# In an attention unit, the turned probabilities are put ahead of the scores two units on, and their low halves ahead of the maximum

## The chip, the core and the metric

One NeuronCore of a Trainium2 chip runs the whole program. It has five engines, each with an instruction stream of its own: TensorE (PE in the rows, its weight loads PEld), VectorE (DVE), ScalarE (ACT), GpSimd (POOL) and SyncE (SP), which here issues the transfers. The engines meet only at semaphores. The metric is the device time of one execution in microseconds. The kernel before takes 1871.24 us, the median of 2 runs (1870.88 to 1871.59).

## What is computed

A graph network on 1250 nodes with 512 features, 21,250 edges: four transformer blocks with attention along the edges, then a two-layer graph convolution. Of the reference, cut to what the change touches:

```python
def _sparse_attention(x, src, dst, wq, bq, wk, bk, wv, bv, wo, bo):
    q = (x @ wq + bq).reshape(N, H, Dh) * Dh ** (-0.5)      # H = 4 heads of Dh = 128
    k = (x @ wk + bk).reshape(N, H, Dh)
    v = (x @ wv + bv).reshape(N, H, Dh)
    scores = jnp.einsum('ehd,ehd->eh', q[src], k[dst])
    smax = jax.ops.segment_max(scores, src, num_segments=N)
    ex = jnp.exp(scores - smax[src])
    denom = jax.ops.segment_sum(ex, src, num_segments=N)
    attn = ex / denom[src]
    out = jax.ops.segment_sum(attn[:, :, None] * v[dst], src, num_segments=N)
    return out.reshape(N, D) @ wo + bo
for i in range(4):
    x = x + _sparse_attention(cond_layer_norm(x), ...)      # the change is here
    x = x + mlp(cond_layer_norm(x))
```

## The kernel before

The edges are turned into a dense 1250 x 1250 table once (how often an edge occurs, as a bias in the logarithm), so that attention is dense: scores plus bias, a softmax along the row, and a product with V. Products are made in three passes from a high and a low half of each operand (fp32r), which is why nearly every tile has a "low half" that VectorE or GpSimd makes by a subtraction.

**Units.** One unit is one head of one tile of 125 query rows. A group G has two tiles and four heads, so 8 units (k = 0 to 7, head k // 2, tile k % 2); a layer has 5 groups, so 40 units, and four layers have 160. What a unit k takes, by engine:

- TensorE, scores: 9 matmuls from q and k into three PSUM banks (`scores`, operands qg and kT, recorded at the helper line L1690).
- VectorE, `score_max`, L1272: adds the bias tile `bt`, writes the sum to SB (pbuf in a few units) and the row maximum to `nmx`, in one custom instruction with a short read of the accumulator behind it.
- ScalarE, `exp_unit`, L870: the exponential of 125x1250 elements, with its row sum `den`.
- VectorE, `normalise`, L1277, L1279, L1281: two instructions on one column (dmx, rden) and the scaling of the 125x1250 probabilities in `P` (pbuf in the rows).
- TensorE, `turn_probs`, L1790: 10 transposes of those probabilities into three further banks.
- ScalarE, `turn_out`, L876: three copies out of these banks, the high half of PT. VectorE, `turn_low`, L1288: three subtractions, the low half.
- TensorE, `attend` (operands PT and V, also L1690): half of a head's 30 matmuls beside each unit; then ScalarE's copy `attn_out` (outTg, L881) and VectorE's `out_low` (outTl, L1294), once per head.

After a group's last head TensorE multiplies with the output weights (`attn_project`, operand WOS), and VectorE adds the two tiles to z (`attn_add`, L1301).

**What sets the order.** Nothing is scheduled automatically: each engine's list is written out by hand, and each engine takes its list in order. All of them work at two units at once: beside unit k, the scores of unit n = k + 2. The five groups of a layer are one loop on each engine (`attn_rest`, then `attn_first` of the next group; four passes) with a start before it and an end, `attn_end`, behind. The waits that matter are few:

```python
# score_max(n): S(n) has been made, and the exponential of unit n-1 has read SB
# normalise(n):
dve.wait_ge(s["exp"], U + 1)            # the exponential of the same unit
# turn_low(k), per piece:
dve.wait_ge(s["Thi"], 3 * U + i + 1)    # ScalarE's copy of the same piece
# scores(n) on TensorE:
pe.wait_ge(s["ttr"], AHEAD + U)         # the maximum of unit n-1 has read the banks
# turn_probs(k) on TensorE:
pe.wait_ge(s["P"], U + 1)               # k is normalised
pe.wait_ge(s["Te"], AHEAD + 3 * U)      # turn_low(k-1) has read the banks
```

ScalarE's list is `turn_out(k)`, `exp_unit(k + 2)` and, at odd k, `attn_out`; the change leaves it alone. VectorE's `attn_end` writes its last units out singly, and has `turn_low` of unit 5 ahead of `score_max` of unit 7 already.

Of the kernel before, what the change touches and what calls it, by code (L numbers as in the profile page):

```python
# [41 lines left out]
UNITS = 2 * H  # L42
# [17 lines left out]
def build(nc, x, src, dst, node_vec1, f_w1, f_b1, f_w2, f_b2, s1_w, s1_b, b1_w, b1_b, wq, bq, wk, bk, wv, bv,  # L60
# [5 lines left out]
    with ExitStack() as ctx:  # L66
# [219 lines left out]
        def settled(eng):  # L286


            eng.sem_inc(s["settled"], 1)
# [743 lines left out]
        def _(dve):  # L1033
# [230 lines left out]
            def score_max(G, U, u, first=False, own=True, banks=ps_S):  # L1264
                dve.wait_ge(s["S"], U + 1)
                dve.wait_ge(s[f"st{u}"], 32 * (G + 1))
                if own:
                    dve.wait_ge(s["exp"], U)
                elif not first:
                    dve.wait_ge(s["Tp"], AHEAD + (3 * (U - 1)))  # L1270
                settled(dve)
                v.tensor_tensor_reduce(out=SB[:, :] if own else P[:, u, :], in0=banks, in1=bt[:, u, :], scale=-1.0, scalar=FLOOR,  # L1272
                                       op0=ALU.add, op1=ALU.min, accum_out=nmx[:, u:u + 1]).then_inc(s["ttr"], 1)

            def normalise(U, u):
                dve.wait_ge(s["exp"], U + 1)
                v.tensor_scalar(dmx[:, u:u + 1], den[:, u:u + 1], 1e-30, None, ALU.max).then_inc(s["dmx"], 1)  # L1277
                dve.wait_ge(s["dmx"], U + 1)
                v.reciprocal(rden[:, u:u + 1], dmx[:, u:u + 1]).then_inc(s["rden"], 1)  # L1279
                dve.wait_ge(s["rden"], U + 1)  # L1280
                v.tensor_scalar(P[:, u, :], P[:, u, :], rden[:, u:u + 1], None, ALU.mult).then_inc(s["P"], 1)  # L1281

            def turn_low(U, h, u):

                for i, (a, b) in enumerate(PIECES):
                    dve.wait_ge(s["Thi"], 3 * U + i + 1)
                    o = PT[:, h % 2, :, a:b, u * T:(u + 1) * T]
                    v.tensor_tensor(o[:, 1], ps_T[0:T, i, 0:(b - a) * T].rearrange("p (t n) -> p t n", n=T),  # L1288
                                    o[:, 0].bitcast(F32), ALU.subtract).then_inc(s["Te"], 1)
# [27 lines left out]

            def unit(G, k, last):
                n = k + 2
                score_max(G + n // UNITS, UNITS * G + n, n % 2, False, not (last and k == 4))  # L1320
                turn_low(UNITS * G + k, k // 2, k % 2)
                normalise(UNITS * G + n, n % 2)

            def attn_first(l, g_):
                for k in range(2):
                    unit(l * NC + g_, k, False)
                    if k == 0:
                        out_low(l * NC + g_ - 1, H - 1)
                attn_add(l, g_ - 1)

            def attn_rest(l, g_):
                for k in range(2, UNITS):
                    unit(l * NC + g_, k, False)
                    if k % 2:
                        out_low(l * NC + g_, k // 2 - 1)

            def attn_end(l, f2):
                G = l * NC + NC - 1
                U = UNITS * G
                for k in range(2, 5):  # L1340
                    unit(G, k, True)
                    if k % 2:
                        out_low(G, k // 2 - 1)
                turn_low(U + 5, 2, 1)
                score_max(G, U + 7, 1, False, False)
                dve.wait_ge(s["zB"], AHEAD + 2 * NC * l + 2)
                front_stats(f2, 0)
                out_low(G, 1)
                turn_low(U + 6, 3, 0)
                normalise(U + 7, 1)  # L1350
                dve.wait_ge(s["Tp"], AHEAD + 3 * (U + 7))
                front_norm(f2, 0)
                out_low(G, 2)
                turn_low(U + 7, 3, 1)
                dve.wait_ge(s["Tp"], AHEAD + 3 * (U + 8))
                front_mod(f2)
                out_low(G, 3)
# [229 lines left out]
        def _(pe):  # L1587
# [182 lines left out]
            def scores(G, U, h, u):  # L1770
                pe.wait_ge(s["qg"], AHEAD + (H * G + h + 1))
                pe.wait_ge(s["ttr"], AHEAD + U)
                for a, b in COLS:
                    e = product(psf[0:T, a:b], lambda i: qg[:, i, h, u * T:(u + 1) * T], lambda i: kT[:, i, h, a:b], True, True)
                e.then_inc(s["S"], 1)
# [7 lines left out]
            def turn_probs(U, u, first=False):  # L1783
                if first:
                    pe.wait_ge(s["ttr"], AHEAD + U + 2)
                pe.wait_ge(s["P"], U + 1)
                pe.wait_ge(s["Te"], AHEAD + 3 * U)
                for p, (a, b) in enumerate(PIECES):
                    for m in range(a, b):
                        e = turn(ps_T[0:T, p, (m - a) * T:(m - a + 1) * T], P[:, u, m * T:(m + 1) * T], ident[0:T, 0:T])  # L1790
                    e.then_inc(s["Tp"], 1)
# [14 lines left out]

            def unit(G, k, last):
                n = k + 2
                if n < UNITS or not last:
                    scores(G + n // UNITS, UNITS * G + n, n % UNITS // 2, n % 2)  # L1810
                turn_probs(UNITS * G + k, k % 2)

            def attn_first(G):

                unit(G, 0, False)
                attend(G - 1, H - 1, 2)
                unit(G, 1, False)
                attn_project(G - 1)

            def attn_rest(G, begun=False):  # L1820
                for k in range(2, UNITS):
                    if begun and k == 2:
                        attend(G, 0, 0)
                        unit(G, k, False)
                    else:
                        unit(G, k, False)
                        attend(G, k // 2 - 1, k % 2)
# [200 lines left out]
```

## Time and profile before

| what | value |
|---|---|
| median of the runs | 1871.24 us (1870.88 to 1871.59) |
| the profiled execution | 1871.84 us |
| its span, first to last instruction | 1870.1 us |
| PE busy | 1810.0 us, 97% |
| PE weight loads busy | 1575.5 us, 84% |
| DVE busy | 1382.6 us, 74% |
| ACT busy | 826.5 us, 44% |
| POOL busy | 453.8 us, 24% |
| granted TensorE clock | 0.996 of full speed |

Busy time is that of instructions on the engine; waiting for a semaphore isn't in it. Attention takes about 214 us in each of the four layers (in the second, from the first maximum at 644.16 us to the last low half of the outputs at 858.19 us).

### The profile page before, as it was taken

The page shows a single profiled execution, that of the slowest core. Times are in us where ns is not written, and L with a number is a line of the kernel's source. Part 1 is how long each engine was busy: PE and PEld are TensorE (multiplying, and loading weights), DVE is VectorE, ACT ScalarE, POOL GpSimd, SP SyncE. Part 2 cuts the span into 40 slices and gives each one's busy share as a digit, 9 for nine tenths or more (in the row PEclk, how much of TensorE's full clock was granted, in tenths as well). Part 3 has the DMA queues.
Part 4 walks back from the last instruction along what each step waited for, and adds up shares of the span by engine and source line. Part 5 has one row for each costly group of instructions (what it writes and reads, how often), then busy time and mean ns, then how long its engine had stood idle before and what let it go on. Part 6 is the DMA issues. An engine that isn't in the chain of part 4 may idle for free. (4 is left out here: it accounts for less than half of the span.)

```text
span 1870.1 us, 33910 instructions
## 1 busy us (share of the span) xinstructions
PE 1810.0 (97%) x11814; PEld 1575.5 (84%) x11814; DVE 1382.6 (74%) x2847; ACT 826.5 (44%) x1613; POOL 453.8 (24%) x547
## 2 busy tenths in 40 slices
PE   6988999999999999999999999999999999999999
PEld 4656988999789889998898899988998999887877
DVE  8996668888875588888754988888549888885431
ACT  1552465555432255554322545544226545536220
POOL 2000333112341341113413411125134111262000
PEclk9999999999999999999999999999999999999999
DMA  4213462110300111113011211040112110522001
GB/s 143 55 41 79 141 176 91 38 43 27 123 24 34 58 42 39 38 31 124 4 54 42 58 38 38 27 128 1 46 50 61 38 38 27 142 72 55 1 1 55
DMA packets 50755, 108.43 MB, mean 58 GB/s; under 512 B 18170, under 2 KB 18222, under 8 KB 50640
## 3 DMA queue, kind: packets, MB, share of 16 engines
q1 hardware_dynamic: 50608, 106.87, 19.7%
q8 instruction: 73, 1.20, 0.3%
q14 instruction: 42, 0.34, 0.1%
q0 software_dynamic: 32, 0.03, 0.0%
HBM read 83.62 MB, written 23.25 MB: 57 GB/s over the span
## 5 line engine op out<-in xcount | busy, mean ns | idle before, releaser
L876 ACT ACTIVATE PT<-ps 125x500 fp32r<-125x500 f32 (+1 forms) x480 | 214.3, 520 | 315.1 <-PE ps L1790 315.1
L1690 PE MATMUL ps<-PT,V 125*128 125x250 f32 x2400 | 313.2, 284 | 1.7 <-DVE PT L1288 1.7
L1690 PE MATMUL ps<-kT,qg 128*125 128x512 f32 (+1 forms) x1440 | 302.1, 354 | 6.3 <-DVE nmx L1272 5.6
L1690 PEld LDWEIGHTS ps<-kT,qg 128*125 128x125 f32 x1440 | 245.4, 186 | 56.0 <-issue 6.9
L1690 PEld LDWEIGHTS ps<-PT,V 125*128 125x128 f32 x2400 | 289.6, 190 | 2.9 <-DVE PT L1288 2.9
L1288 DVE TENSOR_TENSOR PT<-ps,PT 125x500 fp32r<-125x500 f32 (+1 forms) x480 | 253.1, 582 | 2.1 <-ACT PT L876 1.7
L1272 DVE CUSTOM_DVE_ANT_0 SB<-ps,bt 125x1250 f32<-125x1250 f32 x140 | 203.9, 1457 | 47.4 <-PE ps L1690 44.6
L1790 PE MATMUL ps<-ident,pbuf 125*125 125x125 f32 x1600 | 202.2, 273 | 9.9 <-DVE PT L1288 4.0
L1790 PEld LDWEIGHTS ps<-ident,pbuf 125*125 125x125 f32 x1600 | 187.2, 189 | 13.6 <-issue 8.8
L870 ACT ACTIVATE pbuf<-SB,nmx 125x1250 f32<-125x1250 f32 x140 | 188.1, 1344 | 12.1 <-DVE nmx L1272 10.4
L1281 DVE TENSOR_SCALAR pbuf<-pbuf,rden 125x1250 f32<-125x1250 f32 x160 | 150.1, 938 | 5.6
L543 POOL CAST qg<-qc 128x250 fp32r<-128x250 f32 x80 | 36.4, 454 | 443.1 <-PE ps L1690 408.3
L1690 PEld LDWEIGHTS ps<-yTb,wa 128*128 128x128 f32 x1152 | 136.8, 189 | 3.1 <-issue 1.3
L1690 PE MATMUL ps<-yTb,wa 128*128 128x250 f32 x1152 | 137.3, 279 | 1.1 <-DVE yTb L1237 1.1
L1690 PE MATMUL ps<-wmS,hT 128*125 128x512 f32 x480 | 124.3, 403 | 3.8 <-POOL hT L614 3.4
L1632 PE MATMUL ps<-oh_src,oh_dst 125*125 125x512 bf16 (+1 forms) x576 | 115.4, 358 | 6.9 <-DVE oh_src L1116 6.9
L1690 PEld LDWEIGHTS ps<-yT,wmS 128*128 128x128 f32 x960 | 115.6, 191 | 4.2 <-issue 2.4
L1690 PE MATMUL ps<-yT,wmS 128*128 128x250 f32 x960 | 116.0, 280 | 2.0 <-DVE yT L1237 2.0
L1632 PEld LDWEIGHTS ps<-oh_src,oh_dst 125*125 125x125 bf16 x576 | 71.1, 142 | 53.3 <-DVE oh_src L1116 26.0
L1690 PEld LDWEIGHTS ps<-wmS,hT 128*125 128x125 f32 x480 | 84.4, 186 | 32.6 <-POOL hT L614 11.5
L1116 DVE TENSOR_SCALAR oh_src<-iota,edgeT 125x1250 bf16<-125x1250 f16 x192 | 103.7, 540 | 0.0
L1690 PE MATMUL ps<-WOS,outTg 128*125 128x512 f32 x320 | 102.2, 400 | 0.3
(246 smaller groups left out, 2811.6 us busy)
## 6 DMA issues: line engine op xcount, KB each, us to landing
bt<-edge_bias_scratch SPq DMA_DIRECT2D x40, 546.9 KB
q_scratch<-qc SPq DMA_DIRECT2D x16, 500.0 KB, 2.6
qc<-q_scratch SPq DMA_DIRECT2D x16, 500.0 KB, 4.8
counts_scratch<-cblk SPq DMA_DIRECT2D x10, 546.9 KB
c_rows<-counts_scratch SPq DMA_DIRECT2D x10, 546.9 KB
edge_bias_scratch<-b_rows SPq DMA_DIRECT2D x10, 546.9 KB
counts<-counts_scratch SPq DMA_DIRECT2D x10, 546.9 KB
wm<-in_L_gnn_wo_dram SPq DMA_DIRECT2D x4, 1024.0 KB, 8.6
```

What stands on the lines that cost most here:

```text
L543: g.tensor_copy(qg[:, 0, h, :], qc[:, h, :]).then_inc(s["qgh"], 1)
L870: sc.activation(P[:, u, :], SB[:, :] if own else P[:, u, :], ACT.Exp, bias=nmx[:, u:u + 1], scale=-1.0, accum_out=den[:, u:u + 1]).then_in ...
L876: sc.activation(PT[:, h % 2, 0, a:b, u * T:(u + 1) * T], ps_T[0:T, i, 0:(b - a) * T].rearrange("p (t n) -> p t n", n=T), ACT.Copy).then_in ...
L1116: v.tensor_scalar(oh_src[:, slot, :], iota16[:, :], edgeT[:, 0, bass.ds(chunk0 + b, 1)], None, ALU.is_equal).then_inc(s[f"onehot{ring}"], 1)
L1272: v.tensor_tensor_reduce(out=SB[:, :] if own else P[:, u, :], in0=banks, in1=bt[:, u, :], scale=-1.0, scalar=FLOOR, op0=ALU.add, op1=ALU.m ...
L1281: v.tensor_scalar(P[:, u, :], P[:, u, :], rden[:, u:u + 1], None, ALU.mult).then_inc(s["P"], 1)
L1288: v.tensor_tensor(o[:, 1], ps_T[0:T, i, 0:(b - a) * T].rearrange("p (t n) -> p t n", n=T), o[:, 0].bitcast(F32), ALU.subtract).then_inc(s[ ...
L1632: e = mm(psf[0:T, o + a:o + b], oh_dst[:, slot, 0:T], oh_src[:, slot, a:b], start=False, stop=False, skip_group_check=True)
L1690: e = mm(out_, lhs(a), rhs(b), start=start and i == 0, stop=stop and i == 2)
L1790: e = turn(ps_T[0:T, p, (m - a) * T:(m - a + 1) * T], P[:, u, m * T:(m + 1) * T], ident[0:T, 0:T])
```

## The change

Two lines change places, on two engines. On TensorE, beside unit k, the probabilities of k are turned first and the scores of k + 2 made behind them. On VectorE the low halves of unit k are made first, then the maximum of unit k + 2, and directly behind it the normalising of k + 2. No instruction is added or removed, and none changes its shape; waits keep their conditions and move with their instructions.

```diff
@@ VectorE
             def unit(G, k, last):
                 n = k + 2
+                turn_low(UNITS * G + k, k // 2, k % 2)
                 score_max(G + n // UNITS, UNITS * G + n, n % 2, False, not (last and k == 4))
-                turn_low(UNITS * G + k, k // 2, k % 2)
                 normalise(UNITS * G + n, n % 2)
@@ TensorE
             def unit(G, k, last):
                 n = k + 2
+                turn_probs(UNITS * G + k, k % 2)
                 if n < UNITS or not last:
                     scores(G + n // UNITS, UNITS * G + n, n % UNITS // 2, n % 2)
-                turn_probs(UNITS * G + k, k % 2)
```

VectorE in the loop over groups, unit 3, as it stood (L1272 the maximum and its read, L1286 and L1288 the low halves with their waits, L1277 to L1281 the normalising):

```order
L1265 REGISTER_ALU
L1272 ISA SB,nmx<-ps,bt 125x1250
L1272 ISA nmx 125x1
L1286 ISA
L1288 TENSOR_TENSOR PT<-ps,PT 125x4x125
L1286 REGISTER_ALU
L1288 TENSOR_TENSOR PT<-ps,PT 125x4x125
L1286 REGISTER_ALU
L1288 TENSOR_TENSOR PT<-ps,PT 125x2x125
L1277 TENSOR_SCALAR dmx<-den 125x1
L1279 RECIPROCAL rden<-dmx 125x1
L1281 TENSOR_SCALAR pbuf<-pbuf,rden 125x1250
```

The same unit on VectorE now:

```order
L1286 ISA
L1288 TENSOR_TENSOR PT<-ps,PT 125x4x125
L1286 REGISTER_ALU
L1288 TENSOR_TENSOR PT<-ps,PT 125x4x125
L1286 REGISTER_ALU
L1288 TENSOR_TENSOR PT<-ps,PT 125x2x125
L1265 REGISTER_ALU
L1272 ISA SB,nmx<-ps,bt 125x1250
L1272 ISA nmx 125x1
L1277 TENSOR_SCALAR dmx<-den 125x1
L1279 RECIPROCAL rden<-dmx 125x1
L1281 TENSOR_SCALAR pbuf<-pbuf,rden 125x1250
```

The three low halves stood between the read of the maximum and the first instruction of the normalising; now nothing stands there.

TensorE at the head of the loop, unit 2, as it stood (L1772 and L1787 are waits, L1790 the transposes, L1796 and L1798 the waits of the product with V):

```order
L1690 MATMUL ps<-kT,qg 125x512 x6
L1690 MATMUL ps<-kT,qg 125x226 x3
L1786 REGISTER_ALU
L1787 ISA
L1790 MATMUL ps<-ident,pbuf 125x125 x10
L1796 ISA
L1798 ISA
L1690 MATMUL ps<-PT,V 128x250 x15
```

The same on TensorE now:

```order
L1787 ISA
L1790 MATMUL ps<-ident,pbuf 125x125 x10
L1771 ISA
L1772 REGISTER_ALU
L1690 MATMUL ps<-kT,qg 125x512 x6
L1690 MATMUL ps<-kT,qg 125x226 x3
L1796 ISA
L1798 ISA
L1690 MATMUL ps<-PT,V 128x250 x15
```

Transposes, scores, product: the cycle is the same ring of three, with the transposes and the scores exchanged.

## Rows read from the trace of the kernel before

**Rows 1.** The page, busy time by engine: us (share of span) xinstructions

```profile
PE 1810.0 (97%) x11814; PEld 1575.5 (84%) x11814; DVE 1382.6 (74%) x2847; ACT 826.5 (44%) x1613; POOL 453.8 (24%) x547
```

**Rows 2.** Windows: stretch, length, busy PE, PEld, DVE, ACT, POOL, clock, DMA, GB/s

```profile
702.00:744.00 42.00, 42.00 (x298) 38.64 (x297) 35.97 (x71) 22.75 (x45) 6.99 (x10) 1.00 0.15 43
0.00:46.00 46.00, 31.06 (x141) 19.32 (x141) 37.70 (x130) 7.34 (x9) 9.82 (x23) 0.96 0.48 146
```

**Rows 3.** Timeline, VectorE in the loop: start us, us, instruction, [idle before <-releaser]

```profile
701.76 1.46 DVE L1272 CUSTOM_DVE_ANT_0 SB<-ps,bt 125x1250 f32<-125x1250 f32 x1 [1.16 <-PE ps L1690]
703.14 0.08 DVE L1272 DVE_READ_ACCUMULATOR2_ANT nmx<- 125x1 f32 x1
703.14 1.58 DVE L1288 TENSOR_TENSOR PT<-ps,PT 125x500 fp32r<-125x500 f32 x3
704.72 0.15 DVE L1277 TENSOR_SCALAR dmx<-den 125x1 f32<-125x1 f32 x1
705.11 0.87 DVE L1281 TENSOR_SCALAR pbuf<-pbuf,rden 125x1250 f32<-125x1250 f32 x1
...
718.65 1.10 DVE L1281 TENSOR_SCALAR pbuf<-pbuf,rden 125x1250 f32<-125x1250 f32 x1
719.67 0.41 DVE L1294 TENSOR_TENSOR outTl<-ps,outTg 128x250 fp32r<-128x250 f32 x1
720.00 1.44 DVE L1272 CUSTOM_DVE_ANT_0 SB<-ps,bt 125x1250 f32<-125x1250 f32 x1
```

**Rows 4.** Timeline, ScalarE in the same stretch

```profile
703.26 1.34 ACT L870 ACTIVATE pbuf<-SB,nmx 125x1250 f32<-125x1250 f32 x1
...
706.39 1.34 ACT L876 ACTIVATE PT<-ps 125x500 fp32r<-125x500 f32 x3 [1.70 <-PE ps L1790]
```

**Rows 5.** Timeline, TensorE in the same stretch

```profile
704.05 1.87 PE L1690 MATMUL ps<-kT,qg 128*125 128x512 f32 x9
705.76 1.25 PE L1790 MATMUL ps<-ident,pbuf 125*125 125x125 f32 x10
...
708.62 1.89 PE L1690 MATMUL ps<-kT,qg 128*125 128x512 f32 x9
```

**Rows 6.** Timeline, the end of one pass and the start of the next

```profile
735.96 0.71 PE L1690 MATMUL ps<-WOS,outTg 128*125 128x512 f32 x2
...
741.62 1.87 PE L1690 MATMUL ps<-kT,qg 128*125 128x512 f32 x9
742.02 0.69 DVE L1301 TENSOR_TENSOR z<-ps,z 125x512 f32 x1 [1.87 <-PE ps L1690]
...
743.87 1.46 DVE L1272 CUSTOM_DVE_ANT_0 SB<-ps,bt 125x1250 f32<-125x1250 f32 x1 [1.16 <-PE ps L1690]
```

**Rows 7.** Timeline, start of the second layer's attention: unit 3's maximum, exponential, normalising

```profile
657.27 0.08 DVE L1272 DVE_READ_ACCUMULATOR2_ANT nmx<- 125x1 f32 x1
...
657.39 1.34 ACT L870 ACTIVATE pbuf<-pbuf,nmx 125x1250 f32<-125x1250 f32 x1 [1.70 <-DVE nmx L1272]
...
658.85 0.15 DVE L1277 TENSOR_SCALAR dmx<-den 125x1 f32<-125x1 f32 x1 [0.33 <-ACT pbuf L870]
...
660.26 1.45 DVE L1272 CUSTOM_DVE_ANT_0 SB<-ps,bt 125x1250 f32<-125x1250 f32 x1
```

**Rows 8.** Timeline, VectorE at the end of that layer's attention

```profile
827.94 1.46 DVE L1272 CUSTOM_DVE_ANT_0 SB<-ps,bt 125x1250 f32<-125x1250 f32 x1 [1.00 <-PE ps L1690]
...
842.89 1.59 DVE L1288 TENSOR_TENSOR PT<-ps,PT 125x500 fp32r<-125x500 f32 x3 [0.43 <-ACT PT L876]
844.39 1.45 DVE L1272 CUSTOM_DVE_ANT_0 pbuf<-ps,bt 125x1250 f32<-125x1250 f32 x1
```

**Rows 9.** Timeline, TensorE early in the program, three matmuls of one kind twice

```profile
13.82 1.30 PE L1620 MATMUL ps<-zeros 125*125 125x512 bf16 x3 [2.99 <-DVE tab L1093]
...
28.34 0.72 PE L1620 MATMUL ps<-zeros 125*125 125x512 bf16 x3
```

## The prediction, made before the changed kernel had run

> **What bounds the kernel now.** I read the page's busy times first: TensorE at 97%, VectorE at 74% [rows 1]. An average can't say what a reordering is worth, so I went to one pass of the attention loop, 8 units. From the first maximum of one pass at 701.76 [rows 3] to that of the next at 743.87 [rows 6] it takes 42.1 us. In 42.0 us of it TensorE is busy throughout, VectorE 35.97 us [rows 2]. Inside the pass TensorE goes from scores to scores in 708.62 - 704.05 = 4.57 us [rows 5]. VectorE's idle time is spent waiting for it: 1.16 us ahead of the first maximum [rows 3, 6], 1.87 us ahead of the second addition to z [rows 6]. So TensorE sets the pace, and VectorE has 6.0 us of slack in a pass, 0.75 us a unit.
>
> Then I looked at what fills VectorE between a maximum and its own unit's normalising. The read of the maximum is at 703.14, the exponential starts at 703.26 [rows 4], and dmx at 704.72: 1.58 us. The three low halves lie in just this gap, also 1.58 us [rows 3]. That the gap is a wait and not their length is seen at the start of a layer, where no low halves stand there: maximum read 657.27, exponential 657.39, dmx 658.85, again 0.12 + 1.46 = 1.58 us, the last 0.33 us of it idle with the exponential as the releaser [rows 7].
>
> **The change, on VectorE.** It takes the low halves out of that gap and puts them ahead of the maximum. VectorE takes its list in order, so normalising k + 2 waits out the exponential of k + 2 with nothing to do, and the low halves of k + 1 stand behind it. One unit, link by link:
>
> - low halves to maximum: 1.50 us (842.89 to 844.39, where one directly follows the other [rows 8]; each starts 0.08 us before the other ends);
> - maximum to its read: 1.38 us; read to dmx: 1.58 us; dmx to the scaling of P: 0.39 us (704.72 to 705.11) [rows 3];
> - scaling to the next instruction: 0.79 us, its 0.87 less 0.08, the overlap seen at 718.65 (1.10 long, next at 1.02) [rows 3].
>
> That is 5.64 us, against TensorE's 4.57. Eight units are 45.1; a pass also has four low halves of outputs at 0.33 us (719.67 to 720.00 [rows 3]), 1.3, and two additions to z at 0.69 - 0.08, 1.2. Together 47.6 us: VectorE becomes the bound.
>
> **On TensorE** no time is added: transposes, scores and product take the same 4.57 us in the other order, and each finds its input. Turning unit k + 1 needs the low halves of k, done 1.5 us into VectorE's 5.64; the scores need the maximum before, done before that. It idles about 1.1 us a unit, which costs nothing. **ScalarE** copies the turned probabilities of k + 1 only behind the exponential of k + 2. From the exponential's start that is 1.34, plus one piece at 1.34 / 3 = 0.45 [rows 4], and at odd units at most 0.4 for the copy of the outputs: 2.2 us, while VectorE asks for the piece after 1.46 + 0.39 + 0.79 = 2.64. No wait, with 0.4 us to spare.
>
> **At the end of a pass** the cover is thinner. The product with the output weights starts some 0.5 us after the last low half of outputs began and takes 741.62 - 735.96 = 5.66 us [rows 6]. The transposes behind it start at 6.16, ScalarE's first copy 0.63 later (705.76 to 706.39 [rows 4, 5]), ready at some 7.4. VectorE comes to these low halves at 0.33 + 1.50 + 3.35 + 0.79 + 1.22 = 7.2: a wait of 0.2. The scores start 1.0 after the transposes, and the maximum can start 2.25 behind them (741.62 to 743.87 [rows 6]), at 9.4, where VectorE would be at 8.9: 0.5 more. A pass is then 48.3 us, 6.2 more than now.
>
> **Per layer.** Three such passes give 18.6. The first pass now takes 701.76 - 660.26 = 41.5 [rows 3, 7], so it gains 6.8. At its start a maximum followed the scaling at once; now low halves come first: 1.5, the exchange itself. At the end three units run from 827.94 to 844.39, 16.45 us [rows 8]; as changed they are 3 x 5.64 + 0.33 = 17.25, plus 0.8. Behind that point VectorE's list is as it was. Sum 27.7 us, four layers 111 us. The profiled execution's 1871.84 becomes 1982.8, and the median of the runs lies 0.6 below it: **1983 us**.
>
> No queue of transfers is moved past anything. The next group's bias tiles and queries are asked for by the same maxima and scores, now further apart, so they have more time. The granted clock is 1.00 in the pass [rows 2].
>
> **What is least known** is the handover from low halves to maximum, since the row has a maximum of the kind without the wait for SB. From above I bound it by a start 0.10 us after the low halves' end in place of 0.08 us before: 0.18 x 35 units x 4 = 25 us more. I take the row, since the maximum at 720.00, with all its waits, also starts 0.08 us early [rows 3]. From below: without the waits at pass ends, 0.7 x 16 = 11 us less, and 3 less for roundings of 0.02 us a unit. GpSimd's work can stretch the scaling from 0.87 to 1.10 [rows 3]: once a pass, 4 us. So the likeliest case spans 1968 to 2012.
>
> **Rivals.** (1) *The most occupied engine stays the bound.* Place: VectorE's gap behind each maximum. Had the exponential been done when VectorE arrives, or were the wait up to 0.75 us, it would fit into VectorE's slack, and TensorE's 42.1 us a pass would stand: 1871 us. For it: TensorE is 97% busy, and its work is the same. The Trainium skill ("Perfetto Trace Analysis", section "Identifying the Most-Contended Engine") takes the engine with the highest occupancy as the bottleneck, for TensorE by its weight loads, here 84% against VectorE's 74%; by that rule the time would stay at 1871. Against it: the wait is 1.58 us twice over in the rows [rows 3, 7], and 8 x 1.58 = 12.6 us doesn't fit into 6.0. Even if all slack were used, 6.6 us x 16 passes remain. I give it 4%.
>
> (2) *ScalarE's copies come late too.* Place: the low halves of k + 1 wait for the copy behind the exponential. It decides if ScalarE's chain is over 0.4 us longer than the rows add up to. With another 0.4 us in each of 140 units: 56 us, 2039. Against it, the copies and the exponential hold their lengths closely. 6%.
>
> (3) *TensorE, now idle in each unit, loses its clock.* Three matmuls take 1.30 us where they come out of 2.99 us of idling and 0.72 later [rows 9], 1.8 times as long, so at 1.2 GHz in place of 2.4. A pass would be up to 42.1 x 1.8 = 76 us, and 16 passes add up to 540 us: about 2410. It decides if TensorE at 42.1 / 48.3 = 87% busy isn't enough. Against it: in the first 46 us TensorE is busy for 31.06, 68%, at a granted 0.96 [rows 2]. The Trainium skill ("TensorE: Matmul & The Clock Gate", section "Part 1: The HAM clock gate (the "warmup" mystery)") has a unit that watches how busy the array is and gates it to half rate when it idles; by that rule this case is real wherever idling counts as enough. 3%.
>
> **Chances and range.** The likeliest case has 87%. The range 1965 to 2013 takes in its bounds; outside lie rival (3), rivals (1) and (2), and a little of the first case. A run of this kernel tells 2% (37 us) from no change with ease. Faster by over 2%: nothing in attention can go below TensorE's 42.1 us a pass, 1%. Within 2%: rival (1), 4%. Slower by over 2%: 95%.
>
> **What would show it.** In the changed kernel's timeline: dmx 1.58 us behind every read of a maximum, with VectorE idle before it and the exponential as releaser, some 140 times; maxima 5.6 us apart (6.0 across an output's low half) in place of 4.6; a pass of 48 us; TensorE's busy share down to about 92% of the span; a granted clock still at 1.00. Wrong it would be if VectorE had other work in the gap, if the low halves waited for ScalarE in every unit, or if the scores were the late ones: then the wait ahead of the maximum would name TensorE inside the pass and not only at its ends.

## The result, and the profile after

The changed kernel takes **1995.34 us** (median of 2 runs, 1994.56 to 1996.11) against 1871.24 before: a ratio of 1.0667, 95% interval 1.065 to 1.0684. It is slower by 124 us; 1983 was forecast, with a range of 1965 to 2013. The profiled execution has a span of 1992.8 us, 122.7 more than before.

The page's busy times of the changed kernel, in the form of [rows 1]:

```profile
PE 1857.1 (93%) x11814; PEld 1593.9 (80%) x11814; DVE 1376.0 (69%) x2847; ACT 817.2 (41%) x1613; POOL 456.2 (23%) x547
```

Nothing in these shares says that VectorE is now the bound: its share has fallen from 74% to 69%, and TensorE is still the busiest engine. It is so inside a pass too: of the 48.39 us from 742.28 to 790.67, TensorE is busy for 44.86 and VectorE for 35.18. The loop's timeline says what the shares don't. VectorE of the changed kernel, one unit and the start of the next (start us, us, instruction, idle before and releaser):

```profile
705.52 1.45 DVE L1272 CUSTOM_DVE_ANT_0 SB<-ps,bt 125x1250 f32<-125x1250 f32 x1
706.89 0.08 DVE L1272 DVE_READ_ACCUMULATOR2_ANT nmx<- 125x1 f32 x1
708.47 0.15 DVE L1277 TENSOR_SCALAR dmx<-den 125x1 f32<-125x1 f32 x1 [1.50 <-ACT pbuf L870]
...
708.86 0.87 DVE L1281 TENSOR_SCALAR pbuf<-pbuf,rden 125x1250 f32<-125x1250 f32 x1
709.65 1.58 DVE L1288 TENSOR_TENSOR PT<-ps,PT 125x500 fp32r<-125x500 f32 x3
711.14 1.45 DVE L1272 CUSTOM_DVE_ANT_0 SB<-ps,bt 125x1250 f32<-125x1250 f32 x1
```

Between the read of the maximum at 706.89 and dmx at 708.47 lie 1.58 us, as in [rows 3, 7], but now 1.50 us of it are idle, with the exponential as releaser. The low halves come after the scaling, and from maximum to maximum it is 711.14 - 705.52 = 5.62 us, against TensorE's 4.57 before [rows 5]. ScalarE, with the copies of the turned probabilities directly behind the exponential:

```profile
755.37 1.34 ACT L870 ACTIVATE pbuf<-SB,nmx 125x1250 f32<-125x1250 f32 x1 [3.03 <-DVE nmx L1272]
756.61 0.19 ACT L870 ACTIVATION_READ_ACCUMULATOR pbuf<-SB,nmx 125x1 f32 x1
756.70 1.31 ACT L876 ACTIVATE PT<-ps 125x500 fp32r<-125x500 f32 x3
```

TensorE in the same stretch of the loop; its idle time, named in brackets, is what VectorE leaves it:

```profile
754.01 1.35 PE L1790 MATMUL ps<-ident,pbuf 125*125 125x125 f32 x10 [0.83 <-DVE PT L1288]
755.38 1.98 PE L1690 MATMUL ps<-kT,qg 128*125 128x512 f32 x9
```

The waits, summed over the whole program (us in total, times, longest us):

```profile
ACT pbuf L870 <- DVE nmx L1272: 453.1, 152, 5.3
DVE dmx L1277 <- ACT pbuf L870: 211.7, 146, 1.5
PE ps L1790 <- DVE PT L1288: 66.2, 77, 2.0
ACT PT L876 <- PE ps L1790: 59.0, 36, 3.8
```

The second line is the change: 211.7 us of VectorE's time in 146 waits, most of 1.5 us. It is more than the 124 us lost, since before VectorE had slack in every unit, and part of the new wait used that up. The first and third lines are engines waiting for VectorE. ScalarE's long wait for TensorE's transposes, 315.1 us before, has shrunk to 59.0.

The end of a pass, VectorE, to be read beside [rows 6]:

```profile
738.76 1.28 DVE L1301 TENSOR_TENSOR z<-ps,z 125x512 f32 x2
740.20 1.59 DVE L1288 TENSOR_TENSOR PT<-ps,PT 125x500 fp32r<-125x500 f32 x3 [0.16 <-ACT PT L876]
742.28 1.46 DVE L1272 CUSTOM_DVE_ANT_0 SB<-ps,bt 125x1250 f32<-125x1250 f32 x1 [0.49 <-PE ps L1690]
...
790.67 1.46 DVE L1272 CUSTOM_DVE_ANT_0 SB<-ps,bt 125x1250 f32<-125x1250 f32 x1 [0.49 <-PE ps L1690]
```

The two short waits of 0.2 and 0.5 us stand where they were expected, and the pass takes 790.67 - 742.28 = 48.4 us, 42.1 before.

### The profile page after: what moved, and what is told of

It reads as the page before. It is cut to its first block and busy times, and to the rows that moved or that the text cites. A ratio compares the mean times of both kernels' runs of the same rounds, so it can differ in the third digit from the quotient of the medians.

```text
span 1992.8 us, 33910 instructions
## 1 busy us (share of the span) xinstructions
PE 1857.1 (93%) x11814; PEld 1593.9 (80%) x11814; DVE 1376.0 (69%) x2847; ACT 817.2 (41%) x1613; POOL 456.2 (23%) x547
## 5 line engine op out<-in xcount | busy, mean ns | idle before, releaser
L1690 PE MATMUL ps<-kT,qg 128*125 128x512 f32 (+1 forms) x1440 | 317.4, 365 | 4.4 <-DVE nmx L1272 1.9
L1690 PE MATMUL ps<-PT,V 125*128 125x250 f32 x2400 | 303.3, 280 | 1.6 <-DVE PT L1288 1.6
L1790 PE MATMUL ps<-ident,pbuf 125*125 125x125 f32 x1600 | 214.3, 282 | 77.7 <-DVE PT L1288 66.2
L1790 PEld LDWEIGHTS ps<-ident,pbuf 125*125 125x125 f32 x1600 | 192.2, 192 | 97.5 <-DVE PT L1288 44.1
L1288 DVE TENSOR_TENSOR PT<-ps,PT 125x500 fp32r<-125x500 f32 (+1 forms) x480 | 252.8, 582 | 3.3 <-ACT PT L876 2.9
L1272 DVE CUSTOM_DVE_ANT_0 SB<-ps,bt 125x1250 f32<-125x1250 f32 x140 | 203.2, 1451 | 8.7 <-PE ps L1690 8.3
L1277 DVE TENSOR_SCALAR dmx<-den 125x1 f32<-125x1 f32 x160 | 24.6, 153 | 211.7 <-ACT pbuf L870 211.7
L543 POOL CAST qg<-qc 128x250 fp32r<-128x250 f32 x80 | 42.7, 533 | 535.1 <-PE ps L1690 507.5
L1281 DVE TENSOR_SCALAR pbuf<-pbuf,rden 125x1250 f32<-125x1250 f32 x160 | 153.5, 959 | 5.6
```

The lines of the kernel that those rows point to most:

```text
L543: g.tensor_copy(qg[:, 0, h, :], qc[:, h, :]).then_inc(s["qgh"], 1)
L1690: e = mm(out_, lhs(a), rhs(b), start=start and i == 0, stop=stop and i == 2)
```

## The experiments

Each ratio is to the kernel before on the same chip, with its 95% interval. That kernel took 1870.38 us beside e1 to e4 and 1868.69 us beside e5 to e8, so a difference between one of these times and 1995.34 holds to about 3 us.

**One half of the change at a time.** `e1_dve_only` is the VectorE part of the diff alone, `e2_pe_only` the TensorE part alone.

```diff
 # e1, VectorE (TensorE as before)
+                turn_low(UNITS * G + k, k // 2, k % 2)
                 score_max(G + n // UNITS, UNITS * G + n, n % 2, False, not (last and k == 4))
-                turn_low(UNITS * G + k, k // 2, k % 2)
 # e2, TensorE (VectorE as before)
+                turn_probs(UNITS * G + k, k % 2)
                 if n < UNITS or not last:
                     scores(G + n // UNITS, UNITS * G + n, n % UNITS // 2, n % 2)
-                turn_probs(UNITS * G + k, k % 2)
```

> The change on VectorE alone; TensorE keeps scores, then transposes. Theory A (an engine's list is a ring: what stands between a unit's maximum and its normalising is idle time, and each exchange lengthens a ring): VectorE still waits 1.58 us behind each maximum, and the low halves of k, now ahead of the maximum of k+2, also wait for the transposes that TensorE makes only behind the scores. The ring scores 1.71, transposes to ScalarE's copy 0.63, first piece 0.6, low halves 1.50, maximum to its read 1.38 plus 0.1 is 5.9 us a unit, some 50.5 us a pass: 2030 us, slower than both changes together. Rival B (only VectorE's gap counts, TensorE's order doesn't matter): as the whole change, 1995 us. Rival C (TensorE's reordering is what costs): near 1871.

Measured: 2050.15 us, ratio 1.0956 (1.0938 to 1.0974). Slower than both changes together, as theory A had it, and 20 us more than it said. The ring can be read off VectorE, TensorE and ScalarE of e1:

```profile
764.24 1.45 DVE L1272 CUSTOM_DVE_ANT_0 SB<-ps,bt 125x1250 f32<-125x1250 f32 x1
765.61 0.08 DVE L1272 DVE_READ_ACCUMULATOR2_ANT nmx<- 125x1 f32 x1
...
765.75 1.99 PE L1690 MATMUL ps<-kT,qg 128*125 128x512 f32 x9 [1.27 <-DVE nmx L1272]
...
767.57 1.26 PE L1790 MATMUL ps<-ident,pbuf 125*125 125x125 f32 x10
...
768.21 1.34 ACT L876 ACTIVATE PT<-ps 125x500 fp32r<-125x500 f32 x3 [0.79 <-PE ps L1790]
...
768.83 1.59 DVE L1288 TENSOR_TENSOR PT<-ps,PT 125x500 fp32r<-125x500 f32 x3
770.34 1.45 DVE L1272 CUSTOM_DVE_ANT_0 SB<-ps,bt 125x1250 f32<-125x1250 f32 x1
```

Maximum, scores, transposes, copy, low halves, maximum: 1.51 + 1.82 + 0.64 + 0.62 + 1.51 = 6.10 us. The expectation had 5.9. Of the 0.2 us between them 0.11 is that it took the scores at 1.71, their length when they follow other work; behind an idle time they take 1.82 here. A pass is 51.4 us (maxima at 758.14 and 809.52), 50.5 expected. VectorE waits for the exponential as long as in the changed kernel, 211.8 us in all against 211.7, so the 55 us between the two don't lie in that wait but in the longer ring through TensorE.

> The change on TensorE alone; VectorE keeps maximum, low halves, normalising, so there is no gap behind the maximum. Theory A (rings): the maximum of k+2 now waits for scores that stand behind the transposes of k, and the transposes of k+1 wait for the low halves of k, which VectorE makes behind that maximum: transposes 1.01, scores to maximum 2.10, to its read 1.38, low halves 1.50 plus 0.1 is 6.1 us a unit, 51.6 us a pass: 2045 us, with dmx finding the exponential nearly done. Rival B (only VectorE's gap costs): 1871 us. Rival C (the change's whole cost is TensorE's): 1995 us.

Measured: 2077.12 us, ratio 1.111 (1.1092 to 1.1129), the slowest of all, again in A's direction and 32 us over its number. On VectorE of e2 dmx comes 1.58 us behind the read of the maximum, with the low halves in between, and the wait stands ahead of the maximum instead:

```profile
742.63 0.08 DVE L1272 DVE_READ_ACCUMULATOR2_ANT nmx<- 125x1 f32 x1
742.63 1.58 DVE L1288 TENSOR_TENSOR PT<-ps,PT 125x500 fp32r<-125x500 f32 x3
744.21 0.15 DVE L1277 TENSOR_SCALAR dmx<-den 125x1 f32<-125x1 f32 x1
...
747.63 1.46 DVE L1272 CUSTOM_DVE_ANT_0 SB<-ps,bt 125x1250 f32<-125x1250 f32 x1 [2.16 <-PE ps L1690]
```

and on TensorE of e2:

```profile
744.36 1.32 PE L1790 MATMUL ps<-ident,pbuf 125*125 125x125 f32 x10 [1.68 <-DVE PT L1288]
745.45 1.96 PE L1690 MATMUL ps<-kT,qg 128*125 128x512 f32 x9
```

Low halves to transposes 1.73, to scores 1.09, to the maximum 2.18, to its read 1.38: 6.38 us, where 6.1 had been added up, and a pass is 53.0 us, 51.6 expected. So the change isn't a gap on VectorE plus something harmless on TensorE: each half alone makes a longer ring than the two together. With TensorE's half beside it, VectorE's half costs a ring of 5.62 us instead of 6.10.

**Taking the gap away.** `e3_norm_late` leaves both exchanges in and normalises one unit later; the start and the end of a layer are fitted to it (normalising of unit 3 into the loop, that of unit 6 behind the last low halves of unit 5).

```diff
 # VectorE, on the changed kernel
                 turn_low(UNITS * G + k, k // 2, k % 2)
+                normalise(UNITS * G + k + 1, (k + 1) % 2)
                 score_max(G + n // UNITS, UNITS * G + n, n % 2, False, not (last and k == 4))
-                normalise(UNITS * G + n, n % 2)
```

> Both exchanges stay; VectorE normalises unit k+1 between the low halves of k and the maximum of k+2, so its exponential is long done and the 1.5 us gap is gone. Theory A (rings through in-order lists): ScalarE still copies the turned k+1 only behind the exponential of k+2, so the low halves of k+1 now wait: maximum to exponential 1.50, exponential 1.34, first piece 0.6, low halves 1.50, normalising 1.18 is 6.1 us a unit: 2045 us, the wait moved from dmx to the low halves. Rival B (the gap on VectorE is all that costs): VectorE's list is 4.1 us a unit, TensorE's 4.57 us sets the pace again, near 1875 us.

Measured: 2046.16 us, ratio 1.0944 (1.0925 to 1.0962). VectorE's gap is gone and the time has risen by 51 us. The waits of e3 (us in total, times, longest us) show where it went:

```profile
DVE outTl L1294 <- ACT outTg L881: 126.8, 72, 1.8
PE ps L1790 <- DVE pbuf L1281: 122.1, 95, 2.2
DVE PT L1288 <- ACT PT L876: 119.0, 76, 2.0
```

In nearly every unit VectorE now waits for a copy of ScalarE: for that of the output where an output's low half comes first (126.8 us in 72 waits, the largest), else for that of the turned probabilities (119.0 us in 76). Both copies stand in ScalarE's list behind the exponential of k + 2, whose maximum VectorE has only just made. The maxima are 6.10 us apart, 6.1 expected, and 6.37 across an output. Rival B falls: removing the visible wait alone buys nothing.

`e4_norm_exp_late` adds the matching shift on ScalarE; the start and the end of a layer are again fitted to it.

```diff
 # ScalarE, on e3
                 turn_out(UNITS * G + k, k // 2, k % 2)
-                exp_unit(UNITS * G + k + 2, k % 2, not (last and k == 4))
+                exp_unit(UNITS * G + k + 1, (k + 1) % 2)
```

> As the one before, and ScalarE's list shifted too: the exponential of k+1 behind the copies of k, so each copy stands ahead of the next exponential. Theory A: ring of scaling to transposes 0.97, to the copy 0.63, copies 1.34, exponential to dmx 1.46, dmx to scaling 0.39 is 4.8 us a unit, 43.9 us a pass, with a somewhat slower start of each layer: 1912 us, four per cent faster than the change and two slower than before, VectorE no longer idle behind the maximum. Rival B (some other wait of the new order, PSUM banks between transposes and low halves, holds it at 5.6 us or more): 1990 us or over.

Measured: 1911.82 us, ratio 1.0226 (1.0209 to 1.0243), where 1912 was expected. The exponential of the next unit now stands behind the copies:

```profile
770.25 1.45 DVE L1272 CUSTOM_DVE_ANT_0 SB<-ps,bt 125x1250 f32<-125x1250 f32 x1
...
771.20 1.34 ACT L876 ACTIVATE PT<-ps 125x500 fp32r<-125x500 f32 x3 [2.16 <-PE ps L1790]
...
771.82 1.59 DVE L1288 TENSOR_TENSOR PT<-ps,PT 125x500 fp32r<-125x500 f32 x3
...
772.41 1.35 ACT L870 ACTIVATE pbuf<-SB,nmx 125x1250 f32<-125x1250 f32 x1
...
773.88 0.15 DVE L1277 TENSOR_SCALAR dmx<-den 125x1 f32<-125x1 f32 x1 [0.47 <-ACT pbuf L870]
...
775.05 1.45 DVE L1272 CUSTOM_DVE_ANT_0 SB<-ps,bt 125x1250 f32<-125x1250 f32 x1
```

A unit takes 4.80 us, and VectorE waits 0.47 us where it waited 1.50. So the two exchanges need not cost 6.7%: two of the three lists had been moved and the third had not. It is still 2% behind the kernel before, where TensorE's own 4.57 us a unit set the pace.

**Changing the length of the wait.** In `e5_after_exp_half` (on the changed kernel) and `e6_before_exp_half` (on the kernel before) the exponential of 140 units covers 625 of 1250 columns; the rest of each row keeps old values, and the row sum is held at 1 or more.

```diff
+                w = N // 2 if own else N
-                sc.activation(P[:, u, :], SB[:, :] if own else P[:, u, :], ACT.Exp, ...
+                sc.activation(P[:, u, 0:w], SB[:, 0:w] if own else P[:, u, :], ACT.Exp, ...
```

> The changed kernel with the exponential of 140 of the 160 units over 625 of the 1250 columns, and the row sum held at 1 or more; the rest of the row keeps old values. Theory A (VectorE waits out the exponential in every unit): the exponential shortens by some 0.6 us (0.36 us for 250 columns, 1.34 for 1250), the gap from the read of the maximum to dmx from 1.58 to some 0.97, and the time by somewhat less than 140 x 0.61, since the ends of the passes wait for TensorE instead: 1915 us. Rival B (the gap is a fixed handover or the slower pace comes from elsewhere): no more than 5 us off 1995.

Measured: 1929.8 us, ratio 1.0316 (1.0299 to 1.0334); 1915 was expected. The gap shrinks to 1.06 us, as VectorE and ScalarE of e5 show:

```profile
739.99 0.08 DVE L1273 DVE_READ_ACCUMULATOR2_ANT nmx<- 125x1 f32 x1
...
740.11 0.82 ACT L871 ACTIVATE pbuf<-SB,nmx 125x625 f32<-125x625 f32 x1 [2.98 <-DVE nmx L1273]
...
741.05 0.15 DVE L1278 TENSOR_SCALAR dmx<-den 125x1 f32<-125x1 f32 x1 [0.98 <-ACT pbuf L871]
```

That is 0.52 us a unit, not 0.61. 140 x 0.52 would be 73 us; 1995.34 - 1929.8 = 65.5 us are saved. The last unit of a pass gains nothing, since there VectorE waits for the product with the output weights (the last maxima of a pass are 7.70 us apart, at 760.02 and 767.72, and 7.65 to 7.69 in the changed kernel): 16 x 0.52 = 8 us less. (Some 5 us of the 65.5 are another matter: the stretched scalings described below happen to be shorter in e5.) The time follows the exponential's length, so the wait for it is part of VectorE's pace.

> The same shorter exponential in the kernel before, where the low halves fill the gap and TensorE sets the pace. Theory A: nothing gained in the loop, at most some 3 us at the ends of the layers: 1868 to 1871 us. Rival B (the exponential is on the path in both orders): some 80 us less, 1790.

Measured: 1871.34 us, ratio 1.0009 (1.0 to 1.0019): no change. The same work off the same instruction is worth 65.5 us in one order and nothing in the other, since there the low halves cover it.

**Filling the gap.** `e7_gap_filled`: on the changed kernel, `out_low` of a head stands between `score_max` and `normalise`, and ScalarE's `attn_out` ahead of `exp_unit`.

```diff
                 score_max(G + n // UNITS, UNITS * G + n, n % 2, False, not (last and k == 4))
+                if low is not None:
+                    out_low(*low)
                 normalise(UNITS * G + n, n % 2)
```

> The changed kernel with the low half of a head's output put between the read of the maximum and dmx, and ScalarE's copy of it ahead of the exponential. Theory A (work is free in the gap): 0.33 us off VectorE's 5.97 us at four units of a pass, one to two us a pass with the waits at its end: 46.6 us a pass and some 1968 us. Rival B (the copy ahead of the exponential delays it by as much as the gap gives back): no change from 1995.

Measured: 1967.6 us, ratio 1.0526 (1.0508 to 1.0543), 28 us less than the change, where 1968 was expected; a pass is 46.7 us, 46.6 expected. VectorE of e7:

```profile
740.03 0.08 DVE L1269 DVE_READ_ACCUMULATOR2_ANT nmx<- 125x1 f32 x1
740.03 0.41 DVE L1291 TENSOR_TENSOR outTl<-ps,outTg 128x250 fp32r<-128x250 f32 x1
...
741.61 0.15 DVE L1274 TENSOR_SCALAR dmx<-den 125x1 f32<-125x1 f32 x1 [1.17 <-ACT pbuf L870]
```

The low half of the output takes none of VectorE's time here; dmx is still 1.58 us behind the read.

**GpSimd beside the scaling.** `e8_bias_small` leaves out GpSimd's addition of the output bias for all but 2 of 512 columns.

```diff
-                    g.tensor_tensor(z_i, z_i, bob[:, :], ALU.add).then_inc(s["zb"], 1)
+                    g.tensor_tensor(z_i[:, 0:2], z_i[:, 0:2], bob[:, 0:2], ALU.add).then_inc(s["zb"], 1)
```

> The changed kernel with GpSimd's addition of the output bias to z over 2 of 512 columns. Theory A (GpSimd's work stretches VectorE's scaling of P, and VectorE's list now sets the pace): the four scalings of 2.0 us (one per layer, beside this addition in a layer's last pass) go back to 0.87, 4 x 1.15 = 4.6 us less: 1991 us, the other stretched ones stay. Rival B (the stretched scalings are coincidence, or their time is made up elsewhere): 1995 us, and 2.0 us rows stay.

Measured: 1991.43 us, ratio 1.0649 (1.0631 to 1.0666). The 3.9 us to the changed kernel are no more than the two intervals allow by chance, so the rows decide. In the changed kernel, fourth pass of the second layer, GpSimd and then VectorE:

```profile
855.98 5.02 POOL L567 TENSOR_TENSOR z<-z,bob 125x512 f32 x4
```

```profile
859.63 2.04 DVE L1281 TENSOR_SCALAR pbuf<-pbuf,rden 125x1250 f32<-125x1250 f32 x1
```

The same scaling in e8:

```profile
858.11 0.87 DVE L1281 TENSOR_SCALAR pbuf<-pbuf,rden 125x1250 f32<-125x1250 f32 x1
```

That pass takes 48.2 us in e8 and 49.4 in the changed kernel. All four scalings beside this addition are back at 0.87 us; the other stretched ones stay, the longest at 2.00 us.

## Why the prediction held, and where it was 12 us short

**The bound changed as forecast.** VectorE's 5.64 us a unit was added up from five links read off the trace before and measured at 5.62 to 5.64. The pass was 48.3 forecast, 48.4 measured, its two end waits included. The signs named are there: 146 waits of dmx, TensorE's share at 93%; only the granted clock didn't stay at 1.00 throughout. TensorE idles 3.5 us in a pass, where the forecast left it 6.2: its transposes and scores take longer beside the idle times, 1.35 and 1.98 us in the rows above for 1.25 and 1.89 before. (The forecast's last step has a slip: 1982.8 less 0.6 is 1982.2, not 1983.)

**The handover called least known**, low halves to maximum, is 1.49 us (709.65 to 711.14), 1.50 as taken, so the upper bound's 25 us were not needed.

**Too small was the stretched scaling.** I had it once a pass at 0.23 us, 4 us in all, and only in the range. The scalings' busy time over 160 units is 153.5 us where 160 x 0.872 is 139.5: 14.0 us of stretching, in 20 scalings, five of them at 2.0 us. Before it was 10.6 us in 32, most of it covered by TensorE. On the new bound nearly all of it counts: in the second layer 0.93 us in the first pass, 1.17 in the fourth, 0.48 and 0.52 in the end, 3.1 us, and 0.36 more in the start. The second layer's attention takes 31.7 us more than before, where 27.7 had been added up, so stretching is 3.5 of the 4.0 us missed there. The four attentions together take 125.2 us more; the rest of the program takes 2.5 us less, most of it behind the last layer's attention and unexplained, and that gives the 122.7 on the spans against 111 forecast. e8 shows for the largest kind that the stretching comes from GpSimd's work beside the scaling; for the others the trace has only that GpSimd is busy beside each of them.

**The rivals.** (1), the most occupied engine stays the bound, is refuted by e5 and e6: the exponential counts on the path in the new order only. TensorE has the highest share in both kernels, by matmuls (93% against 69%) and by weight loads (80%), and VectorE sets the pace in the loop. The Trainium skill's rule ("Perfetto Trace Analysis", section "Identifying the Most-Contended Engine") names TensorE here, and the measurement goes the other way: an engine that waits in its own list sets the pace at a falling share. (2), ScalarE's copies late in every unit, didn't happen in the change: in the loop the first piece is ready 1.91 us behind the exponential's start and VectorE asks for it after 2.64, or 2.18 and 2.97 beside an output. ScalarE had 0.7 to 0.8 us to spare and not 0.4; the prediction had counted the copy of the output on ScalarE's side and not its low half on VectorE's. e3 shows what the rival's mechanism costs where VectorE does come too early: 2046 us. (3), the clock, happened in spots, below.

**What e1 and e2 missed.** They came out 20 and 32 us above their sums. A pass is 0.9 and 1.4 us longer than added up, 14 and 22 us over 16 passes. The 6 and 10 us that are left are about what falls of the granted clock cost, which no sum had. Five units of e1 hold such a fall. One of them, in the second layer, has its scores at half rate behind a wait of 3.12 us (shown in the last section) and takes 7.74 us; in the first layer the same unit, behind the same wait but without a fall, takes 6.16. Together the five take 7.7 us more than their neighbours. In e2 there are four, one in the first pass of each layer, of 7.8 to 8.9 us where the others take 6.4: 8 us more, with no unit in that place without a fall to compare them with. In both kernels TensorE is on the ring, so a fall costs time at once.

## What to carry to other kernels

When an engine takes its list in order, ask what stands between an instruction and the next one that needs another engine's answer to it: that is cover. Moving it leaves the engine idle for the answer's round trip once per unit, here 1.50 us, and all of that but the engine's slack is lost, whatever its share of busy time. Add up the ring through all lists before moving a step in one of them. Here the exchange costs 9.6% on VectorE's list alone, 11.1% on TensorE's alone, 6.7% on both and 2.3% with normalising and exponential shifted to match. And once an engine becomes the bound, its old disturbances, which had cost little, are part of the price.

## What the runs showed of the hardware

**A scaling of P takes 0.87 to 2.04 us, and which engine starts first goes with it.** e8 shows for GpSimd's addition to z that it is the cause. Being side by side isn't enough: in the changed kernel 62 of the 160 scalings overlap an instruction of GpSimd, and only 20 are stretched. In 18 of these 20 GpSimd had started first, and in the other two it started within 0.04 us of the scaling; of the 42 that kept their 0.87 us, 41 had started before GpSimd. The other side pays then: GpSimd's cast to qg (L543) takes 0.38 to 0.40 us away from a scaling and up to 0.99 us, 0.71 in the median, beside one.

**The granted clock fell behind some waits of about 2 or 3 us, and not under many short ones.** TensorE of the changed kernel idles 0.5 to 0.9 us in every other unit at a granted 1.00, and 44.86 of 48.39 us of a pass are busy. Where the stretched scaling adds its 1.17 us, the idle time becomes 2.01 us, and the transposes behind it take 2.46 us for 1.35:

```profile
863.54 2.46 PE L1790 MATMUL ps<-ident,pbuf 125*125 125x125 f32 x10 [2.01 <-DVE PT L1288]
865.66 2.56 PE L1690 MATMUL ps<-kT,qg 128*125 128x512 f32 x9
```

Windows of 10 us there, first the changed kernel, then e8 without the stretched scaling (busy times of PE, PEld, DVE, ACT, POOL, then clock, share of DMA, GB/s):

```profile
860.00:870.00 10.00, 7.99 (x50) 7.39 (x49) 8.43 (x14) 3.35 (x7) 1.00 (x1) 0.83 0.10 39
```

```profile
860.00:870.00 10.00, 8.59 (x57) 7.45 (x57) 6.86 (x15) 4.81 (x10) 0.00 (x0) 1.00 0.00 0
```

It happens in the last pass of each of the four layers, and once more in the first pass of the first, there too behind a wait of 2.01 us that a stretched scaling had made. From 864 to 866 us the granted clock is 0.50, the lower level of 1.2 GHz. The transposes take 1.8 times as long there. The time didn't suffer: VectorE's next units take 5.62 and 5.96 us, as elsewhere. In e1 one idle time of 3.12 us is followed by scores of 3.11 us in place of 1.99:

```profile
706.42 3.11 PE L1690 MATMUL ps<-kT,qg 128*125 128x512 f32 x9 [3.12 <-DVE nmx L1272]
```

So the third rival has a real mechanism, for a few microseconds at a time. A wait's length doesn't decide it alone. In e1 the clock also fell behind waits of 1.8 us, and the first wait of 3.12 us in the same kernel had no fall behind it:

```profile
285.00 1.95 PE L1690 MATMUL ps<-kT,qg 128*125 128x512 f32 x9 [3.12 <-DVE nmx L1272]
```

The Trainium skill ("TensorE: Matmul & The Clock Gate", section "Part 1: The HAM clock gate (the "warmup" mystery)") says that activity lifts the throttle and idling brings it back; the trace agrees with that where the clock fell, behind waits of 2.01 and 3.12 us, and the row at 285.00 is idling without a fall.
